# Routing stage of a graph and expert network: router weights held still, tiles moved in fours, normalisation on ScalarE

## The reference, cut to what matters

```python
xf = layernorm(x)                      # per node, 512 features, no scale
h = xf @ W_router + b_router           # 512 -> 32 experts
Sm = softmax(h, axis=-1)
G_ek, idx_ek = top_k(Sm.T, k)          # per expert, its k = 312 best nodes
```

## Time and profile before

| what | us |
|---|---|
| median of three executions (3929.16 to 3936.58) | 3929.25 |
| the profiled execution, its own time | 3931.07 |
| its span from the first to the last instruction | 3929.4 |
| first addition (L1024) of the route stage starts at | 943.9 |
| last addition (L1024) of the route stage starts at | 1209.5 |

### The profile page before, as it was taken

One profiled execution on the slowest core, in us unless ns is written; L12 is line 12 of the kernel. 1 busy time (PEld: TensorE's weight loads), 2 busy tenths in 40 slices (PEclk: granted clock), 3 DMA queues, 4 the chain that ended last, 5 costly groups with the idle time before them and its releaser, 6 DMA issues. The chain is left out here.

```text
span 3929.4 us, 61612 instructions
## 1 busy us (share of the span) xinstructions
PE 3238.0 (82%) x18274; PEld 2735.7 (70%) x18275; DVE 2492.0 (63%) x5781; ACT 1346.3 (34%) x2520; POOL 1235.9 (31%) x1606
## 2 busy tenths in 40 slices
PE   6845889997774117999999999999779992969999
PEld 1213667776773107999999999999658882857766
DVE  7855877645676874545445444544278886957776
ACT  4633655421111004444444444444211111114443
POOL 4752532223551002232332322322123320025552
PEclk9977999997555558999999999999889995989999
DMA  4313323335993015544444445444221211146663
GB/s 154 101 25 106 106 91 123 102 123 182 302 304 114 0 22 143 143 104 137 140 99 134 117 126 142 106 132 112 50 87 53 59 43 42 64 121 147 158 158 103
DMA packets 250358, 449.57 MB, mean 114 GB/s; under 512 B 65632, under 2 KB 71073, under 8 KB 249591
## 3 DMA queue, kind: packets, MB, share of 16 engines
q1 hardware_dynamic: 176425, 280.66, 21.8%
q0 software_dynamic: 62368, 145.38, 17.0%
q10 hardware_dynamic: 11318, 20.54, 1.4%
HBM read 319.38 MB, written 126.83 MB: 114 GB/s over the span
## 5 line engine op out<-in xcount | busy, mean ns | idle before, releaser
L1432 PE MATMUL experts_psU<-experts_x_hi,experts_up_hi 128*128 128x312 f32 (+1 forms) x1408 | 442.1, 314 | 21.7 <-issue 15.3
L1461 PE MATMUL experts_psY<-experts_hid_hi,experts_dn_hi 128*128 128x312 f32 (+1 forms) x1408 | 439.3, 312 | 0.0
L1433 PE MATMUL experts_psU<-experts_x_lo,experts_up_hi 128*128 128x312 f32 (+1 forms) x1408 | 435.9, 310 | 0.0
L1434 PE MATMUL experts_psU<-experts_x_hi,experts_up_lo 128*128 128x312 f32 (+1 forms) x1408 | 434.8, 309 | 0.0
L1462 PE MATMUL experts_psY<-experts_hid_lo,experts_dn_hi 128*128 128x312 f32 (+1 forms) x1408 | 431.6, 307 | 0.0
L1463 PE MATMUL experts_psY<-experts_hid_hi,experts_dn_lo 128*128 128x312 f32 (+1 forms) x1408 | 430.1, 305 | 0.0
L1391 POOL DMA_INDIRECT experts_xg<-xn,experts_token_i x96 | 123.2, 1283 | 664.3 <-DVE experts_token_i L1558 644.7
L1597 DVE TENSOR_TENSOR experts_hid_lo<-experts_hid,experts_hid_hi 128x312 fp32r<-128x312 f32 (+1 forms) x352 | 161.3, 480 | 250.7 <-ACT experts_hid L1524 250.7
L1522 ACT ACTIVATE experts_hid_hi<-experts_psU,experts_bup 128x312 fp32r<-128x312 f32 (+1 forms) x352 | 183.3, 521 | 319.2 <-PE experts_psU L1434 317.4
L1432 PEld LDWEIGHTS experts_psU<-experts_x_hi,experts_up_hi 128*128 128x128 f32 (+1 forms) x1408 | 264.4, 188 | 23.2 <-issue 20.5
L1589 DVE TENSOR_TENSOR experts_dn_lo<-experts_dn_raw,experts_dn_hi 128x1536 fp32r<-128x1536 f32 (+1 forms) x128 | 207.9, 1624 | 98.3 <-ACT experts_dn_hi L1500 98.2
(11 more groups left out here) (402 smaller groups left out, 8117.8 us busy)
## 6 DMA issues: line engine op xcount, KB each, us to landing
experts_dn_raw<-in_L_ffn_W_down SPq DMA_DIRECT2D x96, 768.0 KB, 4.6
conv<-gcn_diff SPq DMA_DIRECT2D x120, 256.0 KB, 2.9
experts_up_raw<-in_L_ffn_W_up SPq DMA_DIRECT2D x32, 682.5 KB, 8.5
index_xt<-in_x SPq DMA_DIRECT2D x78, 256.0 KB, 2.7
route_xt<-in_x SPq DMA_DIRECT2D x78, 256.0 KB, 5.0
x<-route_xt SPq DMA_DIRECT2D x78, 256.0 KB, 4.5
xn<-route_xn ACTq DMA_DIRECT2D x78, 256.0 KB, 4.7
two_xt<-x SPq DMA_DIRECT2D x78, 256.0 KB, 2.8
```

Source lines behind the costliest of these rows:

```text
L1432: pe.matmul(acc, up_hi[:, c, cols], x_hi[:, c, :], start=(c == 0), stop=False)
L1433: pe.matmul(acc, up_hi[:, c, cols], x_lo[:, c, :], start=False, stop=False)
L1434: mm = pe.matmul(acc, up_lo[:, c, cols], x_hi[:, c, :], start=False, stop=(c == C - 1))
L1461: pe.matmul(acc, dn_hi[0:w, m, cols], hid_hi[0:w, m, :], start=(m == 0), stop=False)
```

## The change

The buffers of the stage become rings of eight tiles, which two groups of four tiles make up. ACT does the normalisation: POOL computes a shift (minus mean times root) behind each root, and ACT applies both, then starts the DMA of the normalised tile itself. PE holds the router's 32 columns as weights and moves four tiles (512 nodes) past them, four products to a group, which gives sums of shape 32 experts x 512 nodes. DVE adds the bias to these (`bias`), PE transposes them back in blocks of 128 (`turn_back`), and DVE copies the result to `probs` (`take`), both once per group. On DVE the bias is placed five steps, the copy seven steps behind the statistics; on PE `turn_back` stands four steps behind and ahead of `turn`. On SP the store is placed five steps behind and ahead of the load; on POOL the root is three steps behind and ahead of the gather. All four transfers stay.

```diff
-    D, NT, N, R = g.D, g.NT, g.N, 4
+    D, NT, N, R, Q = g.D, g.NT, g.N, 8, 4
...
-        br = ph.sb("br", [P, X])
+        br = ph.sb("br", [X, 1])
...
-            tiles(sp, NT, [(0, load), (2, store)], R)
+            tiles(sp, NT, [(5, store), (0, load)], R)
...
                 pool.tensor_tensor(rstd[:, j:j + 1], mv[:, j, 2:3], g.minus_half[:, 0:1], ALU.pow).then_inc(rooted, 1)
-            tiles(pool, NT, [(0, gather), (2, root)], R)
+                pool.wait_ge(rooted, t * 2 + 1)
+                pool.sem_inc(waited, 1)
+                pool.tensor_scalar(shift[:, j:j + 1], mv[:, j, 0:1], -1.0, rstd[:, j:j + 1],
+                                   ALU.mult, ALU.mult).then_inc(rooted, 1)
+            tiles(pool, NT, [(3, root), (0, gather)], R)
...
             def logits(t, j):
-                at_least(pe, copied, t, 0)
-                at_least(pe, taken, t, 2)
+                if not ends_group(t, j):
+                    return
+                k, n = j // Q, size(t, j)
+                pe.wait_ge(copied, t + 1)
+                if not isinstance(t, int) or t >= R:
+                    pe.wait_ge(biased, group_end(t, j) - R)
                 for c in range(C):
-                    mm = pe.matmul(psR[:, j % 2, 0:X], xT[:, j, c * P:(c + 1) * P], wr[:, c, :],
+                    mm = pe.matmul(psR[0:X, k, 0:n * P], wr[:, c, :], xT[:, k, c, 0:n * P],
                                    start=(c == 0), stop=(c == C - 1))
-                mm.then_inc(routed, 1)
-            tiles(pe, NT, [(0, turn), (1, logits)], R)
+                mm.then_inc(routed, n)
+
+            def turn_back(t, j):
+                if not ends_group(t, j):
+                    return
+                k, n = j // Q, size(t, j)
+                pe.wait_ge(biased, t + 1)
+                if not isinstance(t, int) or t >= R:
+                    pe.wait_ge(taken, group_end(t, j) - R)
+                pe.sem_inc(waited, 1)
+                for q in range(n):
+                    mm = pe.transpose(psB[:, k, q * X:(q + 1) * X], lT[:, k, q * P:(q + 1) * P], g.ident[0:X, 0:X])
+                mm.then_inc(backed, n)
+            tiles(pe, NT, [(4, turn_back), (0, turn), (1, logits)], R)
...
-            def copy(t, j):
+            def norm(t, j):
                 r = node_rows(g, t)
+                at_least(act, rooted, t, 0, 2)
+                at_least(act, turned, t, R)
+                landed(act, nstored, t, j, R, 1)
+                act.activation(xn[:, j, :], xt[:, j, :], ACT.Identity, bias=shift[:, j:j + 1],
+                               scale=rstd[:, j:j + 1]).then_inc(normed, 1)
                 at_least(act, normed, t, 0)
                 act.dma_start(g.xn[bass.ds(t * P, r), :], xn[0:r, j, :]).then_inc(nstored[j], 16)
...
-            tiles(act, NT, [(0, copy)], R)
+            tiles(act, NT, [(2, copy), (0, norm)], R)
...
-            def norm(t, j):
-                at_least(v, rooted, t, 0)
-                at_least(v, turned, t, R)
-                landed(v, nstored, t, j, R, 1)
-                v.tensor_scalar(xn[:, j, :], xt[:, j, :], mv[:, j, 0:1], rstd[:, j:j + 1],
-                                ALU.subtract, ALU.mult).then_inc(normed, 1)
+            def bias(t, j):
+                if not ends_group(t, j):
+                    return
+                k, n = j // Q, size(t, j)
+                v.wait_ge(routed, t + 1)
...
+                v.tensor_scalar(lT[:, k, 0:n * P], psR[0:X, k, 0:n * P], br[:, :], None, ALU.add).then_inc(biased, n)

             def take(t, j):
-                at_least(v, routed, t, 0)
-                if isinstance(t, int) and t == 0:
-                    v.wait_ge(weights, 32)
-                v.tensor_tensor(probs[:, t, :], psR[:, j % 2, 0:X], br[:, :], ALU.add).then_inc(taken, 1)
-
-            tiles(v, NT, [(0, mix), (1, norm), (3, take)], R)
+                if not ends_group(t, j):
+                    return
+                k, n = j // Q, size(t, j)
+                v.wait_ge(backed, t + 1)
+                v.tensor_copy(probs[:, bass.ds(t - n + 1, n), :].rearrange("p t e -> p (t e)"), psB[:, k, 0:n * X])\
+                    .then_inc(taken, n)
+            tiles(v, NT, [(0, stats), (5, bias), (7, take)], R)
```

More of the change, by code:

```diff
@@ L918, in route @@
     TT = probs.shape[1]
+    assert R == 2 * Q
     with Phase(nc, "route") as ph:
         wr = ph.sb("wr", [P, C, X])
-        br = ph.sb("br", [P, X])
+        br = ph.sb("br", [X, 1])
         idx = ph.sb("idx", [P, R, 1], I32)
@@ L925, in route @@
         xn = ph.sb("xn", [P, R, D])
-        xT = ph.sb("xT", [P, R, D])
+        xT = ph.sb("xT", [P, 2, C, Q * P])
+        lT = ph.sb("lT", [X, 2, Q * P])
         st = ph.sb("st", [P, R, 6])
@@ L929, in route @@
         rstd = ph.sb("rstd", [P, R])
+        shift = ph.sb("shift", [P, R])
         most = ph.sb("most", [P, TT])
@@ L933, in route, with ends_group, size, group_end @@
         psR = ph.ps("psR", [P, 2, 512])
+        psB = ph.ps("psB", [P, 2, 512])
         loaded, gathered, stored, nstored = (ph.sems(n, R) for n in ("loaded", "gathered", "stored", "nstored"))
-        weights, staged, mixed, stat_step, rooted, normed, turned, copied, routed, taken, waited = (
-            ph.sem(n) for n in ("weights", "staged", "mixed", "stat_step", "rooted", "normed", "turned", "copied",
-                                "routed", "taken", "waited"))
+        weights, staged, mixed, stat_step, rooted, normed, turned, copied, waited = (
+            ph.sem(n) for n in ("weights", "staged", "mixed", "stat_step", "rooted", "normed", "turned", "copied", "waited"))
+        routed, biased, backed, taken = (ph.sem(n) for n in ("routed", "biased", "backed", "taken"))
         soft, shifted, raised, filled = (ph.sem(n) for n in ("soft", "shifted", "raised", "filled"))
         block = ph.block()
+        def ends_group(t, j):
+            return j % Q == Q - 1 or (isinstance(t, int) and t == NT - 1)
+        def size(t, j):
+            return j % Q + 1
+        def group_end(t, j):
+            return t - j % Q + Q
         @block.sync
@@ L943, in _ @@
             sp.dma_start(wr[:, :, :], W_router.rearrange("(c p) n -> p c n", p=P)).then_inc(weights, 16)
-            sp.dma_start(br[:, :], b_router.partition_broadcast(P)).then_inc(weights, 16)
+            sp.dma_start(br[:, :], b_router.rearrange("(n o) -> n o", o=1)).then_inc(weights, 16)
             def load(t, j):
@@ L1005, in copy @@
                 at_least(act, normed, t, 0)
                 act.dma_start(g.xn[bass.ds(t * P, r), :], xn[0:r, j, :]).then_inc(nstored[j], 16)
+            def copy(t, j):
+                q = j % Q
                 at_least(act, turned, t, 0)
-                at_least(act, routed, t, R)
-                act.copy(xT[:, j, :], psT[:, j % 2, :]).then_inc(copied, 1)
-            tiles(act, NT, [(0, copy)], R)
+                if not isinstance(t, int) or t >= R:
+                    act.wait_ge(routed, group_end(t, j) - R)
+                act.copy(xT[:, j // Q, :, q * P:(q + 1) * P],
+                         psT[:, j % 2, :].rearrange("p (c l) -> p c l", c=C)).then_inc(copied, 1)
@@ L1018, in _, with stats @@
             chain = Chain(v, stat_step, 3)
-            def mix(t, j):
+            def stats(t, j):
                 landed(v, loaded, t, j, R)
                 landed(v, gathered, t, j, R)
-                at_least(v, rooted, t, R)
+                at_least(v, rooted, t, R, 2)
                 v.tensor_tensor(xt[:, j, :], xt[:, j, :], gt[:, j, :], ALU.add).then_inc(mixed, 1)
@@ L1028, in mix @@
                 chain.end()
-            def norm(t, j):
-                at_least(v, rooted, t, 0)
-                at_least(v, turned, t, R)
-                landed(v, nstored, t, j, R, 1)
-                v.tensor_scalar(xn[:, j, :], xt[:, j, :], mv[:, j, 0:1], rstd[:, j:j + 1],
-                                ALU.subtract, ALU.mult).then_inc(normed, 1)
-            def take(t, j):
-                at_least(v, routed, t, 0)
-                if isinstance(t, int) and t == 0:
-                    v.wait_ge(weights, 32)
-                v.tensor_tensor(probs[:, t, :], psR[:, j % 2, 0:X], br[:, :], ALU.add).then_inc(taken, 1)
-            tiles(v, NT, [(0, mix), (1, norm), (3, take)], R)
+            def bias(t, j):
[3 more added lines that the diff above has]
+                v.wait_ge(routed, t + 1)
+                if isinstance(t, int) and t == Q - 1:
+                    v.wait_ge(weights, 32)
+                if not isinstance(t, int) or t >= R:
+                    v.wait_ge(backed, group_end(t, j) - R)
+                v.tensor_scalar(lT[:, k, 0:n * P], psR[0:X, k, 0:n * P], br[:, :], None, ALU.add).then_inc(biased, n)
+            def take(t, j):
+                if not ends_group(t, j):
[5 more added lines that the diff above has]
+            tiles(v, NT, [(0, stats), (5, bias), (7, take)], R)
             step = Chain(v, soft)
```

## The result

The changed kernel takes 3938.24 us (median of 11 executions, 3931.44 to 3943.97), beside 3929.55 for the kernel before on the same chip: a ratio of 1.002, 95% interval 1.0011 to 1.0029, so +8.7 us. Measured again on another occasion it was 3942.15 us and 1.0033 (1.0021 to 1.0045). The forecast was 3939. The total is right; the terms behind it are not all right, and part of the agreement is luck.

The account below looks back on a forecast made before the run. A loop of three gathers through POOL's queue was taken to pace the route stage; spacing +5.9 us and tail +3.9 us gave +9.8 on the profiled execution's 3931.07, on the median 3939 us; range 3914 to 3963.

Parts of the forecast that it names:

- the loop of three gathers: Route stage: gather stands behind the root three tiles earlier on POOL's queue, so three at most; 9.36 us, 3.12 a tile.
- one in three: Route stage before: DVE sat idle for the gather ahead of 24 of 79 additions, 40.2 us in all.
- What bounds the changed kernel: Route stage after: the loop at 3.28 us a tile plus 0.20 of meetings, 3.48, so +5.9 us.
- meetings: Queues of the route stage holding each other up: 0.285 us a tile before, 0.20 after.
- The shift: POOL, between root and next gather: 0.21 us of wait and 0.26 of work, 0.47 us on the loop.
- The ring: Buffers of eight tiles: allow more gathers than POOL's queue issues, depth stays three; longer loop body booked at none.
- DVE's relief: DVE's work falls from about 2.7 to 2.2 us a tile; nothing booked beyond the smaller meeting cost.
- The tail: Last addition to softmax, 9.6 us before: +0.3 us at 2.4 GHz, +7.4 at 1.2 GHz, middle +3.9 taken.
- The bound by transfers: Part of rival "nothing to tell": 1.05 MB a tile at 302 GB/s takes 3.47 us; 3929 to 3936, chance 0.32.
- PE never became the bound: Rival: PE at 1.2 GHz holds up DVE's bias and the additions, about 3.65 us a tile, 3955; chance 0.12.
- Evening out: Rival: DVE's relief removes the 0.285 of meetings, stage runs at POOL's 3.2 us a tile, 3914; chance 0.21.
- What POOL meets: POOL's instructions take longer beside DVE's addition: its copy 0.18 to 0.745 us; only the addition clearly seen to hold it.

## Why the prediction was right, point by point

*What bounds the kernel*: the loop of three gathers. Right for the kernel before: with rings of eight, moving the root alone took the additions from 3.226 to 2.861 apart. That "one in three" additions waited was no evidence for it, since that count left out the 16 under "issue". That the DMA share of 0.91 is no bound is shown by the run with a second store, at 365 GB/s, and by this one, at 359 with the same four transfers.

*What bounds the changed kernel*: 3.48 was the loop's 3.28 and 0.20 of meetings. The runs show POOL's own queue, 3.3 us a tile, and 0.1 to 0.2 of waiting for statistics. The prediction had POOL's own work at 3.12, as its lower end; gather, copy and shift are each longer than it took, by 0.04, 0.04 and 0.13 us. Loop and queue lie so near that five gathers gain only 0.12 to 0.17 a tile in the changed kernel. So the number is right, and the path to it only in part.

*The shift*: 0.47 us on the loop, 0.16 a tile; measured 0.16 and 0.19. The size is right. It is 0.39 long instead of 0.26, because it meets DVE's addition, so with its wait 0.60. Both kernels with the shift on POOL leave POOL some 0.2 us a tile of waiting for statistics, so these runs don't tell whether it costs as a third of the loop or by filling POOL's queue.

*The ring.* That it allows no more gathers than POOL's queue issues is right. That it is worth nothing is not, in the kernel before: -0.137 a tile, -10.7 us, from one profile, with the cause open. Whether it is worth as much in the changed kernel, where SP's order differs too, no run shows.

*DVE's relief*, booked at 0.085 a tile (0.285 of meetings to 0.20): not seen. The changed kernel with the shift on DVE runs at 3.281, the kernel before with rings of eight at 3.226. The +0.055 between them holds the shift's 0.21 us on DVE and is less than two profiles can differ by, so it shows neither a relief nor its absence. Something takes back half of the shift's 0.16 to 0.19, since 0.08 is left. The ring is one candidate. The gather's landing is another: 5.4 and 5.5 us after 5.7 and 6.0, about 0.13 a tile on a loop of three, where the prediction put nothing. That the sum came to +5.9 for +6.2 is in part luck.

*The tail*: +3.9 forecast. From the last addition to the softmax 10.6 us in one profile, 11.9 in the other, after 9.7: +0.9 and +2.2. Most of the gap to my figure is PE's clock. Here is the end of the first, PE and DVE:

```profile
1207.84 4.77 PE L1017 MATMUL route_psR<-route_xT,route_wr 128*32 128x512 f32 x8
...
1214.36 2.77 PE L1017 MATMUL route_psR<-route_xT,route_wr 128*32 128x384 f32 x8 [0.37 <-ACT route_xT L1051]
...
1217.23 0.60 DVE L1082 TENSOR_SCALAR route_lT<-route_psR,route_br 32x384 f32<-32x384 f32 x1 [2.83 <-PE route_psR L1017]
...
1218.72 2.79 DVE L1095 TENSOR_REDUCE route_most<-probs_probs 128x79 f32<-128x2528 f32 x1
```

A group of 512 columns takes 4.77 us: I gave 3.9 at the higher level and 7.9 at the lower one, and the records of this group start 0.86 us apart at first and 0.43 at the end, so the clock changes over within it. The last group runs at the higher level, 2.77 for my 2.9. The wait of the last tiles for the group before, as worked out for the lower level, is there, but shorter.

*Other stages*, put at nothing without a word: some 2 us in the top-two stage, within what that stage varies by. The sum of what was measured is 6.2 for the spacing, 1.6 for the tail and 2.2 for that stage, less 0.9 for a first addition that comes sooner after the stage's first gather (4.2 and 5.4 us, after 5.5 and 5.8): +9.1. The four profiled executions themselves differ by 9.9 in the mean, the medians by 8.7 and 13.0.

*The rivals.* The bound by transfers fell with the second store. PE never became the bound: DVE did not wait for it at the bias in the changed kernel's loop. Evening out can't be read from DVE's waits, whose names differ between the profiles; the end that it would have gone to, POOL's 3.2, was out of reach, since POOL needs 3.3.

*What POOL meets.* POOL's copy went from 0.27 to 0.22 us on average and the root from 0.64 to 0.59, but the shift is 0.39, after 0.26 in the top-two stage. Two shifts of the first profile after, without and with an addition beside them:

```profile
1005.14 0.26 POOL L991 TENSOR_SCALAR route_shift<-route_mv,route_rstd 128x1 f32<-128x1 f32 x1 [0.21 <-POOL route_rstd L988]
...
1012.16 0.69 DVE L1067 TENSOR_TENSOR route_xt<-route_xt,route_gt 128x512 f32<-128x512 f32 x1 [1.12 <-POOL route_rstd L988]
1012.21 0.77 POOL L991 TENSOR_SCALAR route_shift<-route_mv,route_rstd 128x1 f32<-128x1 f32 x1 [0.21 <-POOL route_rstd L988]
```

Of its 79 shifts the 41 beside which no addition ran took 0.26 to 0.27 us; the others took up to 0.81. So the addition, with two inputs from SBUF, is what holds the shift. The Trainium skill (GPSIMD Engine Reference, Specifications) names that kind of instruction and those in a two-port mode; the trace agrees on the first, and for the second no run here separates it.

## What to carry to other kernels

The depth of a prefetch is what the issuing queue's order allows, not what the ring holds: write down which instruction stands in front of each gather, follow its wait, and divide the loop's time by the number of tiles under way. Then add up each engine's own work and waits on itself for a tile: the longest of these sums is what is left when the loop is lifted, here POOL's 3.3 or 3.1 and DVE's 2.9, and not the transfers. A term can be read as off the path and still count, as the longer ring did, so test such a term by itself. And a time taken off an engine that waits gives only more waiting.

## What the runs showed that was not expected

The same experts code ran with four or with eight pauses of PE of some 4 us, "issue" in the profile, as the program ahead of it differed: four in the kernels before, with the shift and in all that hold the change (13.6 to 16.1 us in all), eight in the two kernels before with rings of eight (27.9 and 29.3). With eight the stage is some 19 to 20 us longer, 12 to 14 of them in the pauses themselves, which outweighs what the ring brings. That the place of the code decides is a guess; no run moved the code alone. The top-two stage shows a smaller effect of the kind, 424 to 429 us over the fourteen profiles. And a change of 8 us was within what one profile of each kernel can hide: the additions were 3.32 and 3.41 us apart in two profiles of the kernel before.
